# All rope operations on VectorE, spread over six routed turns per piece

## The reference

```python
xn = _layernorm(x)
# attention: q and k are turned by their position before the scores
q = (xn @ Wq + bq).reshape(B, S, H, D);  k = (xn @ Wk + bk).reshape(B, S, H, D)
q = _apply_rope(q, cos, sin);            k = _apply_rope(k, cos, sin)   # x * cos + x_rot * sin
...
# feed-forward: 64 experts, 6 per token, and two shared ones
topk_w, topk_ids = jax.lax.top_k(softmax(xn @ gate_w.T), 6)   # weights normalised to a sum of 1
act = silu(g) * u;  routed = sum over the 6 experts of weight * (act @ w_down[e])
out = x + attention(xn) + routed + shared
```

## Time and profile before

| | us |
|---|---|
| time, median of 3 runs | 646.74 (646.31 to 649.73) |
| profiled execution, its own time | 650.96 |
| its span, first to last instruction | 649.1 |
| TensorE busy | 615.3 (95%) |
| VectorE busy | 430.5 (66%) |
| ScalarE busy | 307.2 (47%) |
| GpSimd busy | 321.0 (49%) |

### The profile page before, as it was taken

One profiled execution on the slowest core, in us unless ns is written; L12 is line 12 of the kernel. 1 busy time (PEld: TensorE's weight loads), 2 busy tenths in 40 slices (PEclk: granted clock), 3 DMA queues, 4 the chain that ended last, 5 costly groups with the idle time before them and its releaser, 6 DMA issues.

```text
span 649.1 us, 17796 instructions
## 1 busy us (share of the span) xinstructions
PE 615.3 (95%) x4929; PEld 364.3 (56%) x4929; DVE 430.5 (66%) x1366; ACT 307.2 (47%) x802; POOL 321.0 (49%) x340
## 2 busy tenths in 40 slices
PE   6999999998998999998999999999999899999987
PEld 3644455654554555554555555555554566666654
DVE  6768688557664665667665565544446788899865
ACT  3643131033443444444444544444445777777752
POOL 4000000268636775567765686564300776766662
PEclk9999999999997999999999999999999999999999
DMA  9610011138978768996799977996425777777432
GB/s 297 179 30 2 0 34 34 57 103 255 283 228 278 232 190 247 320 334 185 213 298 295 315 222 235 327 327 134 102 59 193 210 232 229 227 227 232 129 109 74
DMA packets 78167, 124.52 MB, mean 192 GB/s; under 512 B 11113, under 2 KB 52618, under 8 KB 78090
## 3 DMA queue, kind: packets, MB, share of 16 engines
q1 hardware_dynamic: 43098, 60.18, 30.4%
q0 software_dynamic: 15872, 46.16, 24.4%
q10 hardware_dynamic: 19120, 17.18, 7.8%
HBM read 85.73 MB, written 37.75 MB: 190 GB/s over the span
## 4 chain that ended last, share of the span: by engine, by line
PE 80%; DVE 6%; DMA 3%; issue 3%; ACT 3%; POOL 2%; DVEq 1%; SPq 0%; ACTq 0%; POOLq 0%
PE pair L1216 23%; PE pair L1243 14%; PE pair L1186 6%; PE pair L1173 5%; PE pair L1121 4%; PE bank L1227 4%; PE bank L1330 4%; PE bank L1200 3%; PE bank L1362 2%; PE pair L1083 2%; DVE negm L985 2%; DMA lower<-xn_rows,idx_all 2%; PE pair L1292 2%; PE pair L1312 1%; PE bank L1341 1%
## 5 line engine op out<-in xcount | busy, mean ns | idle before, releaser
L454 POOL DMA_INDIRECT lower<-xn_rows,idx_all x128 | 138.0, 1078 | 221.8 <-DVE idx_all L958 107.8
L1216 PE MATMUL pair<-space,work 128*64 (+1 forms) x768 | 167.4, 467 | 6.3 <-DVE wqkv_sb L932 3.7
L1243 PE MATMUL pair<-lower,work 88*64 x512 | 121.5, 379 | 0.7 <-ACT lower L615 0.7
L1216 PEld LDWEIGHTS pair<-space,work 128*64 128x64 f32 x768 | 67.4, 138 | 78.4 <-issue 66.9
L874 DVE TENSOR_TENSOR work<-work,pair 128x176 f32<-128x176 f32 x128 | 42.9, 337 | 101.5 <-ACT work L609 100.7
L1243 PEld LDWEIGHTS pair<-lower,work 88*64 88x64 f32 x512 | 69.6, 137 | 48.7 <-issue 18.0
L1216 PE MATMUL pair<-wqkv_sb,work 128*64 128x352 f32 x256 | 90.6, 477 | 0.0
L615 ACT ACTIVATE lower<-pair 128x256 f32<-128x256 f32 x128 | 49.1, 384 | 76.5 <-PE pair L1243 76.5
L519 POOL DMA_INDIRECT wqkv_sb<-y_rows,slot_i x48 | 48.1, 1002 | 58.2 <-DVE negm L985 33.2
L602 ACT ACTIVATE work<-pair 128x256 f32<-128x256 f32 x128 | 42.6, 381 | 66.9 <-PE pair L1173 41.3
L985 DVE TENSOR_REDUCE negm<-pair 128x2 f32<-128x256 f32 (+1 forms) x128 | 64.6, 549 | 9.5 <-PE pair L1292 7.5
(11 more groups left out here) (205 smaller groups left out, 1156.5 us busy)
## 6 DMA issues: line engine op xcount, KB each, us to landing
space<-wgu SPq DMA_DIRECT2D x66, 352.0 KB
y_rows<-lower ACTq DMA_DIRECT2D x128, 128.0 KB, 4.3
qk_all<-qk_rows SPq DMA_DIRECT2D x64, 256.0 KB
lower<-wdn SPq DMA_DIRECT2D x64, 176.0 KB
qk_rows<-qk_all POOLq DMA_DIRECT2D x32, 256.0 KB, 5.7
qk_rows<-space POOLq DMA_DIRECT2D x16, 256.0 KB, 4.0
xn_rows<-qk_all SPq DMA_DIRECT2D x16, 128.0 KB, 1.9
lower<-xn_rows,idx_all POOLq DMA_INDIRECT x128
```

The source lines that it names most:

```text
L454: po.indirect_dma_start(xg[:, r % XB, :], None, xn_rows[:, :], bass.IndirectOffsetOnAxis(idx_all[:, r:r + 1], 0)).then_inc(xg_in[r % XB], 16)
L1216: last = pe.matmul(pair[u % 2][strip, 0:2 * F], xgT[u][:, c, strip], n, start=c == 0, stop=c == EC - 1, skip_group_check=True)
L1243: last = pe.matmul(pair[u % 2][strip, 512:512 + E], hT[:, u % 2, c, strip], n, start=c == 0, stop=c == 1, skip_group_check=True)
```

## The change

GpSimd keeps only the gathers and the stores. VectorE does all nine operations of all eight pieces, in the order of the pieces, one piece in six turns: in each turn one operation stands ahead of the turn's first gate product, and in every other turn a second one stands at the turn's end. The two `slot_weights` operations move from behind the second gate product to between the two. The stores of piece n follow the gathers 24 + 12n to 24 + 12n + 7, one store behind each gather.

```diff
+PIECE_TURNS = 6
+STORES_FROM = 2 * PIECE_TURNS + 12
...
             for r in range(RT):
                 gather(r)
-                while r >= XB and r % 2 and done < (r - XB + 1) * todo // (RT - 4 * XB) and done < todo:
-                    piece(*steps[done])
-                    done += 1
-            assert done == todo
+                n, j = (r - STORES_FROM) // (2 * PIECE_TURNS), (r - STORES_FROM) % (2 * PIECE_TURNS)
+                if 0 <= n < PIECES and j < 2 * COPIES:
+                    piece(n, j)
...
-                    po.wait_ge(turned_ok if a else roped, ROPE_STEPS * (n // 2 + 1))
+                if j == 0:
+                    po.wait_ge(turned_ok, ROPE_STEPS * (n + 1))
...
-            def turn_keys(n, k):
+            def turn_piece(n, k):
...
-                if n > 1 or k:
-                    dve.wait_ge(turned_ok, ROPE_STEPS * (n // 2) + k)
+                if n or k:
+                    dve.wait_ge(turned_ok, ROPE_STEPS * n + k)
...
+                piece, j = (i // 2 - 1) // PIECE_TURNS, (i // 2 - 1) % PIECE_TURNS
+                steps = list(range(j * ROPE_STEPS // PIECE_TURNS, (j + 1) * ROPE_STEPS // PIECE_TURNS)) if 0 <= piece < PIECES else []
+                for k in steps[:1]:
+                    turn_piece(piece, k)
                 for n in (i + 2, i + 3):
                     if n == 1:
                         up_copy(2, 2)
                     if n < TILES:
                         hidden(n, n % XB)
-                if 0 <= i // 2 < PAIRS * NT:
-                    slot_weights(i // 2)
-                if 0 < i // 2 <= PIECES // 2 * ROPE_STEPS:
-                    turn_keys((i // 2 - 1) // ROPE_STEPS * 2 + 1, (i // 2 - 1) % ROPE_STEPS)
+                    if n % 2 == 0 and 0 <= i // 2 < PAIRS * NT:
+                        slot_weights(i // 2)
+                for k in steps[1:]:
+                    turn_piece(piece, k)
```

More of the change, by code:

```diff
@@ L95 @@
 COPIES = 4
-PIECE_STEPS = ROPE_STEPS + 2 * COPIES
+PIECE_TURNS = 6
+STORES_FROM = 2 * PIECE_TURNS + 12
 HIGH_IN = ((0, 1), (0, 2))
@@ L279, in build @@
         w_loaded = [sem("w_loaded_even"), sem("w_loaded_odd")]
-        gu_own = sem("gu_own"); dn_own = sem("dn_own"); idx_col = sem("idx_col"); po_turn = sem("po_turn"); roped = sem("roped"); turned_ok = sem("turned_ok");
+        gu_own = sem("gu_own"); dn_own = sem("dn_own"); idx_col = sem("idx_col"); turned_ok = sem("turned_ok");
         table_set = sem("table_set"); table_at = sem("table_at"); bias_at = sem("bias_at"); bias_ok = sem("bias_ok"); tables_in = sem("tables_in")
@@ L455, in gather, with piece @@
                                       bass.IndirectOffsetOnAxis(idx_all[:, r:r + 1], 0)).then_inc(xg_in[r % XB], 16)
-            def piece(n, k):
+            def piece(n, j):
                 g, a, u = n // 2, n % 2, n % BUFS
[L460 to L463, removed]
-                        po.wait_ge(turned_ok if a else roped, ROPE_STEPS * (n // 2 + 1))
[L465 to L493, removed]
@@ L495, in _ @@
-            po.wait_ge(qkv_ok, len(order))
-            po.wait_ge(tables_in, 1)
+                i, x = j // 2, j % 2
+                if j == 0:
+                    po.wait_ge(turned_ok, ROPE_STEPS * (n + 1))
+                at = qk_rows.rearrange("(h i x d) a t -> h i d x a t", h=H, i=COPIES, x=2)
+                src = spare[u] if i in HIGH_IN[a] else qT[:, g, a]
+                po.dma_start(at[:, i, :, x, a, g * SPAN_T:(g + 1) * SPAN_T], src[:, x]).then_inc(rows_out[u], 16)
             po.wait_ge(idx_ok, 1)
@@ L498, in _ @@
             po.wait_ge(xn_out, 16 * NT)
-            steps = [(n, k) for n in range(PIECES) for k in range(ROPE_STEPS if n % 2 else 0, PIECE_STEPS)]
-            todo = len(steps)
-            done = 0
             for r in range(RT):
                 gather(r)
-                while r >= XB and r % 2 and done < (r - XB + 1) * todo // (RT - 4 * XB) and done < todo:
-                    piece(*steps[done])
-                    done += 1
-            assert done == todo
+                n, j = (r - STORES_FROM) // (2 * PIECE_TURNS), (r - STORES_FROM) % (2 * PIECE_TURNS)
@@ L886, in slot_weights @@
                 i.then_inc(dpair, 1)
-            def turn_keys(n, k):
-                g, u = n // 2, n % BUFS
-                q, other = qT[:, g, 1], spare[u]
-                if n > 1 or k:
-                    dve.wait_ge(turned_ok, ROPE_STEPS * (n // 2) + k)
+            def turn_piece(n, k):
+                g, a, u = n // 2, n % 2, n % BUFS
+                q, other = qT[:, g, a], spare[u]
+                if n or k:
+                    dve.wait_ge(turned_ok, ROPE_STEPS * n + k)
                 else:
@@ L898, in turn_keys @@
                     dve.wait_ge(rows_out[u], 16 * 2 * COPIES * (n // BUFS))
-                cos, sin = (table[:, 1, cs].unsqueeze(1).to_broadcast([P, SPAN_T // S, S]) for cs in range(2))
+                cos, sin = (table[:, a, cs].unsqueeze(1).to_broadcast([P, SPAN_T // S, S]) for cs in range(2))
                 def batches(z):
```

## The result

| | before, us | after, us |
|---|---|---|
| median of 4 runs each | 648.24 (646.31 to 651.80) | 638.29 (637.63 to 639.61) |
| profiled execution, its own time | 650.96 | 637.95 |
| its span | 649.1 | 636.1 |

The ratio of the times is 0.9835, with a 95% interval of 0.9805 to 0.9866: faster by 1.3 to 2.0%, 10 us between the medians. The change was forecast to give 14.4 us and 632.3; the time lies inside the range of 628.5 to 640, 6 us above the forecast.

The account below looks back on a forecast made before the run. TensorE's products were taken as the floor, 5.275 us a turn, with 15.43 us lost in five places to GpSimd's ropes and store wait. Less 1.0 added, 14.4 us off the 646.74 median gives 632.3, range 628.5 to 640.

Parts of the forecast that it names:

- the five places: Routed turns at GpSimd's four q pieces, plus one long turn where GpSimd's store waits for VectorE: 15.43 us lost, all removed.
- Sum on the profiled execution: 15.43 us removed less 1.0 added gives 14.4: span from 649.1 to 634.7, time from 650.96 to 636.5.
- The upper bound of 6: Crowded DMA in the store stretches: the new store order costs between 0 and 6 us, taken as 1.
- The same sum on the median gives 632.3: Median 4.2 us below the profiled time, so the 14.4 us gain is taken from 646.74.
- A rope ahead of the first gate product is free: VectorE's 0.61 us rope fits the 0.62 us wait for ScalarE's silu before that product; cost taken as 0.
- The upper bound of 13 us for a rope held up by the register load: Longest wait, 1.9 us, delays the copy 0.54 us in each of 24 two-operation turns.
- Room at the end of the turn: After the second gate product, the next copy can begin 0.32 or 0.93 us earlier; TensorE needs it only at 195.51.
- The case given 0.72: Full gain less small change: 629 to 636 us, chance 0.72.
- the next, given 0.17: Part of the gain given back or the long turn staying: 636 to 643.5 us, chance 0.17.
- Part of the gain given back: Rival: late gathers or copies lose 6 to 13 us, so 637 to 644; shares chance 0.17 with the long turn staying.
- The DMA queues as the cause of the longest turn: Rival: that turn's 5.9 us stay, time 638; shares chance 0.17 with part of the gain lost.
- Ropes and gathers locking each other: Rival: gathers hold VectorE's ropes, copies come late in 24 turns, 19 to 34 us lost, 651 to 666; slower 0.05.

Follow-up runs that it names:

- the first repeat: The kernel before, unchanged, profiled a second time: 646.41 us, 12.1 us lost above the floor.
- the repeats: The kernel before, unchanged, profiled twice more, one run each: 646.41 and 646.06 us, 12.1 and 11.6 us lost above the floor.

## Why the prediction was right, and where its size was off

- **What bounds the kernel, and the causes of the five places.** Right. The places went from 15.43 to 0.57 us above the floor. That GpSimd's computing blocks VectorE is shown by the added idle products, and that the store's wait makes the longest turn by the later and the earlier stores.
- **Sum on the profiled execution.** Forecast: its time goes from 650.96 to 636.5. Measured 637.95, 13.0 us of the 14.4. The added cost was taken as 1.0 for the stores; the turns outside the five places lose 3.12 us after, where they lost 1.74 before (0.5 in the first repeat), so 1.4 to 2.6 were added, and 0.57 remain in the places: this term of the sum was too small. The upper bound of 6 held it, but the reason was wrong: the order of stores does not matter, and with a register load of TensorE moved the loss is gone.
- **"The same sum on the median gives 632.3".** This step failed, and it carries most of the miss: 4.6 of the 6.0 us. It took the 4.2 us between the profiled time and the median of before as there in the changed kernel too, whose median is 0.3 above its profile. Of the 4.2, 1.5 was chance of three runs: a fourth moved their median from 646.74 to 648.24. The rest lies in the stalls removed, which are not the same in each execution: in the first profile's longest turn the clock fell for some 7 us, in the repeats not at all. The five places sum to 11.66 us in the first repeat (2.53, 2.75, 3.07, 2.21, 1.10). With 0.57 left in the places and 2.6 added that is a gain of 8.5, which is the difference of the two executions, 646.41 - 637.95. The medians differ by 10.0, between that and the 13.0 of the first profile. The repeats show that what differs lies inside the turns that change: they are 4.6 and 4.9 us faster than the first profile and lose 5.0 and 5.6 us less there. A faster execution lacks part of the very stalls that the change removes.
- **A rope ahead of the first gate product is free.** Right, with more room than claimed: two fit. The upper bound of 13 us for a rope held up by the register load did not come.
- **Room at the end of the turn.** The prediction compared the copy's end with the product's start and took what lay between, 0.5 us, as room. With both ropes at the end the product starts 0.41 us after the copy's end. The step was wrong without harm to the change, as the change moves the copy earlier in the earlier trace rows's turn or leaves it.
- **Rivals.** The case given 0.72, 629 to 636, did not come; the time lies in the next, given 0.17, and the range held only by its upper part. Part of the gain given back, at 637 to 644: the time lies there, but by smaller stalls more than by late gathers or copies. The DMA queues as the cause of the longest turn would also have given 638, so the time alone speaks as much for them as for my causes; the list of turns and the stores four gathers later refute them. Ropes and gathers locking each other did not occur, at 0.69 against 0.68 us.
- **What would show it.** Marks 5.27 to 5.4 us apart hold for most turns, not for seven between 5.48 and 6.35. All ten long turns are among the turns that have two operations or, behind the last rope, by their place would have them: a pattern of two, which the prediction named as a sign of being wrong. But the ropes are not its cause: the last long turn, at 419.86, comes after the last rope, and with the ropes in place and the register load moved no turn is long any more. No store waits; slot weights are at 279 ns; the routed part ends 13.5 us earlier. VectorE's waits for the silu fell by 52 us in all, more than 48 ropes of 0.61; the slot weights now stand in the wait between the products too.

Open: which part of a register load holds TensorE back (the load itself, or the first product that uses the register), why that falls on every second turn, and what the gaps ahead of the transposes in the kernel before are. The runs with moved loads show only that the place between the two tiles' down products is what costs in the changed kernel. Nor do the parts add up: the store's wait (6.9 us), GpSimd's computing (14.6) and the place of the ropes (some 7) were each changed alone, and together they are more than the 10 us of the change. What the move of the slot weights gave by itself was not tried.

## What to carry to other kernels

Take the stalls that a change is to remove from more than one execution before you sum them: the same stall lowered the clock here in one execution and not in the next, and the difference between a profiled time and the median may lie in those very stalls. In an in-order queue that also prefetches, give every instruction that waits for another engine a full turn of slack, and ask on both sides, as a store that comes too late holds up the writer of its buffer instead (4.29 us here). When the large waits are gone, look at what stands between an engine's products without a releaser: moving one register load a turn out of that place was worth the last 4 us here, and next to nothing in the kernel before, where the gaps lay elsewhere. And when a copy's end is set against the start of the product that uses it, take off the handoff (0.40 us here) before calling the rest room.

## What the runs showed of the hardware

- The granted clock fell to 0.50 in the longest turn in two of four profiles with the same stall at the store, behind 3.17 and 2.72 us of TensorE's waits, and stayed at 1.00 behind 2.30 and 1.53; the fall cost nearly as much as the wait itself. Beside idle products on GpSimd it fell behind 0.98 and 0.61 us.
- A VectorE copy that ended at 221.34 us was used by a product at 221.75, 0.41 us later, with no releaser in the profile; 14 of 18 such handoffs in that run took 0.40 us.
- Each of 36 idle GpSimd products of 1.29 us cost the kernel about 0.4 us, mostly by VectorE instructions beside it: a slot weight took 1.14 us on average and not 0.28, the rope shown 2.02 us; a gate product with one input from `pair` did not grow (0.33 us).
